# Who adds the position bias: half of every second key unit against all of every fourth

## The reference, cut to what matters

```
qkv    = xn @ Wqkv.T                       # per sequence: 512 x 768
logits = q @ k.T * 16**-0.5 + pos_bias     # 16 heads of 512 x 512
attn   = softmax(logits)
out    = (attn @ v) @ Wout.T
x      = x + out + experts(xn)
```

## Time and profile before

| | |
|---|---|
| median of three runs | 1942.63 us |
| the profiled execution | 1945.23 us, of which the traced span is 1943.6 us |
| attention of layer 1 in the trace | about 1172 to 1740 us of the span |
| busy over the whole span | PE 89%, DVE 59%, ACT 54%, POOL 52% |

### The profile page before, as it was taken

One profiled execution on the slowest core, in us unless ns is written; L12 is line 12 of the kernel. 1 busy time (PEld: TensorE's weight loads), 2 busy tenths in 40 slices (PEclk: granted clock), 3 DMA queues, 4 the chain that ended last, 5 costly groups with the idle time before them and its releaser, 6 DMA issues. The chain is left out here.

```text
span 1943.6 us, 32399 instructions
## 1 busy us (share of the span) xinstructions
PE 1729.3 (89%) x11015; PEld 1131.9 (58%) x11015; DVE 1139.9 (59%) x2512; ACT 1050.0 (54%) x1443; POOL 1007.3 (52%) x763
## 2 busy tenths in 40 slices
PE   4889888887899999999999976888888888878998
PEld 3455555554688888888888763343343334326556
DVE  5665666663233534335344537988888888846345
ACT  2555555555633323233232323998889889885543
POOL 2344443342334444344343444998889889874202
PEclk7999999998999999999999986999999999988999
DMA  4333333322621211012011263232322223117347
GB/s 128 89 110 92 87 92 92 108 77 75 198 88 60 72 35 60 26 58 82 26 59 36 61 209 130 72 93 66 88 88 86 85 71 109 34 58 265 111 153 232
DMA packets 119263, 182.86 MB, mean 94 GB/s; under 512 B 14198, under 2 KB 73078, under 8 KB 119163
## 3 DMA queue, kind: packets, MB, share of 16 engines
q1 hardware_dynamic: 112812, 173.21, 29.3%
q10 hardware_dynamic: 5712, 6.29, 1.0%
q0 software_dynamic: 640, 2.10, 0.3%
HBM read 90.72 MB, written 39.91 MB: 67 GB/s over the span
## 5 line engine op out<-in xcount | busy, mean ns | idle before, releaser
L878 POOL TENSOR_TENSOR l_prob<-l_prob,l_bias 128x1024 f32<-128x1024 f32 x192 | 452.3, 2381 | 57.1 <-ACT l_prob L1036 56.3
L1323 POOL TENSOR_TENSOR f_hl<-f_full,f_hh 128x512 fp32r<-128x512 f32 x192 | 247.9, 1291 | 401.3 <-DVE f_hh L1361 273.6
L1098 DVE CUSTOM_DVE_ANT_0 l_slot<-l_slot,l_bias 128x512 f32<-128x512 f32 x512 | 339.5, 714 | 26.5 <-PE l_slot L1183 26.4
L1039 ACT ACTIVATE l_prob<-l_prob 128x1024 f32<-128x1024 f32 x256 | 273.1, 1076 | 0.1
L523 DVE TENSOR_REDUCE l_peak<-l_slot 128x2 f32<-128x256 f32 (+3 forms) x256 | 206.1, 821 | 111.0 <-PE l_slot L615 108.6
L1411 PE MATMUL f_ps<-f_hh,f_hi_h 128*128 128x512 f32 x1024 | 260.6, 390 | 3.3 <-ACT f_hh L1335 2.6
L1411 PE MATMUL f_ps<-f_hl,f_hi_h 128*128 128x512 f32 x1024 | 258.3, 389 | 0.0
L411 ACT ACTIVATE l_prob<-l_slot 128x1024 f32<-128x1024 f32 (+3 forms) x256 | 175.1, 706 | 94.9 <-PE l_slot L634 91.9
L1411 PEld LDWEIGHTS f_ps<-f_hh,f_hi_h 128*128 128x128 f32 x1024 | 191.9, 188 | 47.4 <-issue 3.3
L350 POOL TENSOR_SCALAR_AFFINE_SELECT l_prob<-l_prob 128x256 f32<-128x256 f32 x256 | 105.2, 417 | 212.9 <-ACT l_prob L411 210.1
L1411 PEld LDWEIGHTS f_ps<-f_hl,f_hi_h 128*128 128x128 f32 x1024 | 192.2, 188 | 39.9
(11 more groups left out here) (229 smaller groups left out, 2774.9 us busy)
## 6 DMA issues: line engine op xcount, KB each, us to landing
l_stacks<-l_parts SPq DMA_DIRECT2D x372, 128.0 KB, 2.6
f_raw<-in_L_ffn_h_w SPq DMA_DIRECT2D x16, 512.0 KB, 4.2
f_raw<-in_L_ffn_h_w SPq DMA_DIRECT2D x32, 256.0 KB, 2.6
e_w<-in_L_ffn_f SPq DMA_DIRECT2D x32, 256.0 KB, 2.9
l_bias<-ext SPq DMA_DIRECT2D x16, 448.0 KB, 8.4
attn<-l_out_sb ACTq DMA_DIRECT2D x9, 512.0 KB, 2.9
l_x_in<-in_L_attn_x SPq DMA_DIRECT2D x8, 512.0 KB, 3.9
xh<-l_xh SPq DMA_DIRECT2D x8, 512.0 KB, 2.6
```

The costliest lines, as they stand in the source:

```text
L878: return eng.tensor_tensor(probs(n), src, bias[:, h:h + 2, j * P:j * P + T], ALU.add)
L1039: act.activation(probs(n), probs(n), ACT.Exp).then_inc(p_exp.sem, 1)
L1098: ins = dve.tensor_tensor_reduce(src, src, bias[:, 4 * g + 2 * pr + a, t * P:t * P + T], 1.0, 3 * NEG, ALU.add, ALU.max, peak[:, g, a, pr, ...
L1323: pool.tensor_tensor(t.hl[layer % 2][:, o], t.full[:, n % 2], t.hh[layer % 2][:, o].bitcast(F32), ALU.subtract).then_inc(self.h_lo.sem, 1)
```

## The change

DVE now takes part in every second key unit (odd n), for the second of the two heads only. ACT copies only the first head of such a unit, POOL adds the bias to that head only, and DVE reads the second head from PSUM, adds and stores it. Even units go over ACT and POOL as a whole. So unit `n % 4 == 1` changes from DVE alone to a half each, `n % 4 == 3` from ACT and POOL alone to a half each, and even units stay. The counts of the semaphores change with it: an odd unit's slot is released by ACT's copy and DVE's addition both (two waits on TensorE), and its exponential waits for POOL's and DVE's additions both (two waits on ACT).

```diff
-    def pooled(n):
-        return n % 4 != 1
-
-    def added(n):
-
-        return (p_pooled, n // 4 * 3 + (0, 0, 1, 2)[n % 4] + 1) if pooled(n) else (p_added, n // 4 + 1)
+    def heads_by_pool(n):
+
+        return 1 if n % 2 else 2

     def released(kind, k):

         if kind == "prob":
-            return (p_copied, added(k)[1]) if pooled(k) else added(k)
-        return LAST_READ[kind], 2 if kind == "v" else k + 1
+            return [(p_copied, k + 1)] + ([(p_added, k // 2 + 1)] if heads_by_pool(k) == 1 else [])
+        return [(LAST_READ[kind], 2 if kind == "v" else k + 1)]
...
-    def add_bias(eng, n, src):
+    def add_bias(eng, n, src, first, last):

         g, j, pr = prob_of(n)
         h = 4 * g + 2 * pr
-        return eng.tensor_tensor(probs(n), src, bias[:, h:h + 2, j * P:j * P + T], ALU.add)
+        return eng.tensor_tensor(probs(n)[:, first:last], src[:, first:last],
+                                 bias[:, h + first:h + last, j * P:j * P + T], ALU.add)
...
# POOL
-                if kind == "prob" and pooled(n):
+                if kind == "prob":
                     if n % 8 == 0 and opening(b):
                         pool.wait_ge(bias_in[n // 8].sem, 16 * 4)
-                    wait(pool, p_copied, added(n)[1], b)
-                    add_bias(pool, n, probs(n)).then_inc(p_pooled.sem, 1)
+                    wait(pool, p_copied, n + 1, b)
+                    add_bias(pool, n, probs(n), 0, heads_by_pool(n)).then_inc(p_pooled.sem, 1)
...
# ACT
-                    if pooled(n):
-                        wait(act, b_ps, n + 1, b)
-                        act.copy(probs(n), slot(kind, n)[:]).then_inc(p_copied.sem, 1)
+                    wait(act, b_ps, n + 1, b)
+                    some = heads_by_pool(n)
+                    act.copy(probs(n)[:, 0:some], slot(kind, n)[:, 0:some]).then_inc(p_copied.sem, 1)
                 if kind == "prob_exp":
-                    wait(act, *added(n), b)
+                    wait(act, p_pooled, n + 1, b)
+                    if heads_by_pool(n) == 1:
+                        wait(act, p_added, n // 2 + 1, b)
                     act.activation(probs(n), probs(n), ACT.Exp).then_inc(p_exp.sem, 1)
...
# DVE
-                if kind == "prob" and not pooled(n):
+                if kind == "prob" and heads_by_pool(n) == 1:
                     wait(dve, value_ps, n // 2 + 1 - RING, b)
                     wait(dve, b_ps, n + 1, b)
-                    add_bias(dve, n, slot(kind, n)[:]).then_inc(p_added.sem, 1)
+                    add_bias(dve, n, slot(kind, n), 1, 2).then_inc(p_added.sem, 1)
...
# TensorE, claim
-                        wait(pe, *released(before, k), bb)
+                        for tally, count in released(before, k):
+                            wait(pe, tally, count, bb)
```

More of the change, by code:

```diff
@@ L748, in biased_attention @@
     b_ps, p_exp = sem("b_ps", STEPS), sem("p_exp", STEPS)
-    p_copied, p_pooled, p_added = sem("p_copied", STEPS * 3 // 4), sem("p_pooled", STEPS * 3 // 4), sem("p_added", STEPS // 4)
+    p_copied, p_pooled, p_added = sem("p_copied", STEPS), sem("p_pooled", STEPS), sem("p_added", STEPS // 2)
     value_ps, o_copied, ot_ps = sem("value_ps", QUADS * TT), sem("o_copied", QUADS), sem("ot_ps", QUADS)
```

## The result

The changed kernel takes 1949.49 us (median of 16 runs), the kernel before 1943.20 (16 runs): ratio 1.0031, 95% interval 1.0018 to 1.0043. It is slower, by little more than can be told from no change; 1922 was forecast, range 1906 to 1943. The profiled execution took 1950.5 us.

What follows compares the result with a forecast made beforehand. Four engines at 86 to 90%, none full, wait for each other, PE for PSUM slots; terms -20.7 + 0 + 0 + 0 = -20.7 us take the median 1942.6 to about 1922 us, range 1906 to 1943.

Steps and rivals of the forecast that it cites:

- (a): Units n % 4 == 1: DVE's shorter addition returns the PSUM slot 0.53 us earlier, 20.7 us off PE's idle.
- (b): Units n % 4 == 3: slot 0.30 us earlier or 0.42 later; 11 us gained to 13 lost, taken as 0.
- (c): DVE's load: 1.3 us more a sequence, inside its 8.8 us of idle, counted as nothing; 10 us if uncovered.
- Rival 2: Units n % 4 == 3: DVE's half additions delay maxima, 4.9 us a sequence; slower, 1951 us; chance 0.13.

Runs made afterwards that it cites:

- a_only: Changed kernel with only units n % 4 == 1 split; at n % 4 == 3 DVE adds nothing and one head's bias is left out: 1934 us.
- a_relief: a_only with ACT also taking the exponential of the first head alone in units n % 4 == 1: 1933 us.
- b_only: Changed kernel with units n % 4 == 1 whole on DVE again, only n % 4 == 3 split: 1976 us.
- after_again: Changed kernel itself, run again beside others on the same chip: 1950.5 us.
- after_fill: Changed kernel with PE making score unit 8's products three times over, in the hole behind unit 27: 1948 us, 1.0025 of the kernel before.
- after_no27: Changed kernel with unit 27 not split, ACT and POOL taking both heads: 1945.8 us.
- even_halves: Changed kernel with the half additions in even units instead of odd ones: 1938 us.
- after_max: Changed kernel with the maxima's transposition issued behind the value products in steps 9 and 17: 1933 us.
- before_max: Kernel before the change, with the maxima's transposition issued behind the value products in steps 9 and 17: ratio 0.9973.
- even_max: even_halves with the maxima's transposition issued behind the value products in steps 9 and 17: 1933 us.
- even14: even_halves with units 14 and 16 not split, ACT and POOL taking both heads: 1942 us.

## Why the prediction was wrong

(a) held for the wait that it was about. Expected: 2.6 us a sequence off the units n % 4 == 1; measured 2.4 in their pairs of steps, and PE's idle before the score products fell by 18 us where 20 were named. Alone it is worth less: a_only won 0.7 us a sequence and a_relief 1.6, at a higher load of ACT than in the changed kernel. The prices held too: POOL's half addition took 1.29 us, not the 1.11 that follows from the Trainium skill's cycles an element (GPSIMD Engine Reference, section 3.1); POOL never held up an exponential.

The steps that failed are (b) and (c), both taken as 0; together they cost 2.5 us a sequence, 20 us over the eight, which is the whole of the forecast gain. (b) was bounded by the right row: it had the slot 0.42 us late behind placed work, and at units 11 and 23 it came 0.46 and 0.44 late. But it was taken as the middle of gain and loss, and the gain of 0.30 us at the other units did not show: the slot came earlier by more than 0.04 us at unit 27 alone, by 0.25 us, and that pair still took 0.44 longer, because the maxima were late. Of the 2.5 us lost, the pairs from 11, 23, 7 and 31, where the slot came later, hold 1.4, and those from 3, 19 and 27, where it did not, 1.1. (c) charged DVE's added load against its idle time in the sum and found it covered. b_only shows otherwise: with 6.4 us of idle left on DVE its sequence is 2.9 us longer, and its pairs from n % 4 == 3 take 35.0 us as in the changed kernel (34.8), for DVE's work in those pairs delays what PE needs next. Rival 2 had this mechanism, its price (4.9 us a sequence) and its tipping point (53% reaching PE); 2.5 / 4.9 is 51%. It was given 0.13, on the argument that DVE is relieved by as much in the other pairs. That relief is the gain already counted in (a), and the delay here comes on top.

That alone gives no change: +0.1 us a sequence, 1 us in all. The other 5 us go with the clock, which no step of the prediction had. The first seven sequences took 482.9 us in the trace before, 486.5 in the changed kernel's and 487.6 in after_again's: 3.6 and 4.7 us more, of which the periods explain about 1. So half or more of the missing 5 us lies in this stage, and the falls of the clock there are what differs (14 us at the lower level against 27 in both). What is shown of their cause: they come most often where PE is emptiest, the change made that place emptier, filling it removes them there (after_fill), and runs without the half addition there are 4.7 us faster at an unchanged period (after_no27). What is not: how much of the 0.005 of clock stems from that place. b_only has the hole as large and fell there once in seven sequences, even_halves has it as before and never fell, and after_no27's trace, without the added hole, has as much time at the lower level as the changed kernel's, at units 4 and 12 instead.

The rule of the Trainium skill that was weighed (VectorE: DVE Perf Modes, the errata section: many small instructions pay the fixed latency more often) points to the right sign but not to the cause: even_halves has the same small instructions and is faster than the kernel before. No run here tests it by itself: a_only and a_relief show that ACT's load counts, but there ACT copies more elements too.

## What to carry to other kernels

Idle time in an engine's sum does not cover added work; its place in that engine's order does or does not. Before moving work onto a fixed-order engine, ask at each place what it issues next and who waits for that, and price late results beside freed ones. Where TensorE waits with ready products behind the waiting instruction, reorder those first: here that was worth more than the change (16 us off the changed kernel, 4 off the kernel before).

## What the runs showed of the hardware

A recurring hole in TensorE's work can cost clock in a kernel whose TensorE is busy for 85% of the time and more. With PE busy 2.23 of 4.10 us and its longest wait there 1.4 us, the clock fell to its lower level at that place in four of the first seven sequences, in both traces of the changed kernel; with the hole closed (after_max, before_max, even_max) in none of the seven. The hole alone does not decide it: in b_only, with PE busy 2.27 of 4.10 us, it was one in seven, and in even_halves, with the hole of the kernel before, none.

Across repeated runs of one kernel the clock varied by up to 0.014 (b_only, 0.945 to 0.959), and one run of before_max at 0.914 stands outside that; 0.001 goes with 0.8 to 1.5 us in most kernels. Kernels with periods 0.2 us apart (even14 and even_halves, run on different chips) came out in the reverse order. Part of this arises ahead of the changed stage: over the 20 traces its first key products start between 1189.7 and 1198.2 us, after nearly the same work.

For fp32 elements the halves cost more than half: 1.29 us against 2.38 for POOL's addition, 0.68 against 1.22 for DVE's, 0.60 against 1.02 for ACT's copy.
